# Last attention of a graph network layer on one core: GpSimd adds the probabilities of two units, and TensorE takes their sums over sources once for both

## The reference

```python
H, D = (8, 32)                                   # heads, features of a head
h = (feat @ W.T).reshape(N, H, D)
e = einsum('ehd,ehd->eh', h[src], h[dst]) / sqrt(D)
m = segment_max(e, dst, num_segments=N)
ex = exp(e - m[dst])
s = segment_sum(ex, dst, num_segments=N)         # the sum over sources
out = segment_sum(h[src] * (ex / s[dst])[:, :, None], dst, num_segments=N)
```

## Time and profile before

| what | value |
|---|---|
| median of 3 runs | 6491.18 us |
| the profiled execution, its own time | 6495.75 us |
| its span | 6493.9 us |
| TensorE busy, of the span | 5235.9 us (81%) |
| VectorE | 3690.0 us (57%) |
| ScalarE | 1601.6 us (25%) |
| GpSimd | 3034.0 us (47%) |
| the last attention in the trace | 5424 to 6137 us |

### The profile page before, as it was taken

One profiled execution on the slowest core, in us unless ns is written; L12 is line 12 of the kernel. 1 busy time (PEld: TensorE's weight loads), 2 busy tenths in 40 slices (PEclk: granted clock), 3 DMA queues, 4 the chain that ended last, 5 costly groups with the idle time before them and its releaser, 6 DMA issues.

```text
span 6493.9 us, 83030 instructions
## 1 busy us (share of the span) xinstructions
PE 5235.9 (81%) x25932; PEld 3282.1 (51%) x25932; DVE 3690.0 (57%) x7654; ACT 1601.6 (25%) x2625; POOL 3034.0 (47%) x2048
## 2 busy tenths in 40 slices
PE   4677777777699898989569798776657998998899
PEld 3555555555455575558557566761113333222366
DVE  6777777787511202120235400979986997777732
ACT  1111111111222201220132121245541003555421
POOL 2577777788888878877777885000000000000000
PEclk8887887788799988999788699989988999999889
DMA  7765565644555596559799766944340001222100
GB/s 172 171 119 109 110 120 114 94 65 64 57 20 15 8 124 41 15 23 125 90 159 112 56 48 61 206 105 120 105 115 28 28 24 46 72 73 70 53 17 25
DMA packets 537605, 515.96 MB, mean 79 GB/s; under 512 B 262861, under 2 KB 494230, under 8 KB 531390
## 3 DMA queue, kind: packets, MB, share of 16 engines
q1 hardware_dynamic: 275694, 422.98, 29.8%
q0 software_dynamic: 261696, 90.13, 22.6%
HBM read 359.18 MB, written 153.71 MB: 79 GB/s over the span
## 4 chain that ended last, share of the span: by engine, by line
PE 46%; DVE 13%; issue 6%; SPq 5%; DMA 3%; ACT 1%; DVEq 0%; POOL 0%; ACTq 0%; POOLq 0%; PEldq 0%
PE PS L909 6%; PE PS L881 6%; PE PS L2033 6%; SPq L187 5%; PE PS L1901 5%; DVE WORK L1785 4%; PE PS L1270 4%; DVE MXS L1942 4%; PE PS L892 4%; PE PS L1562 3%; PE PS L1061 2%; PE PS L1050 2%; PE PS L245 2%; PE PS L1922 1%; PE PS L1252 1%
## 5 line engine op out<-in xcount | busy, mean ns | idle before, releaser
L642 POOL DMA_INDIRECT pairs<-PAIR_CNT,PAIR_IDX x1364 | 2159.8, 1583 | 559.1 <-issue 438.9
L469 DVE SCALAR_TENSOR_TENSOR XT<-PS,ROWS,XT 128x512 f32<-128x512 f32 (+1 forms) x1364 | 937.6, 743 | 148.1 <-PE PS L461 137.7
L999 DVE SCALAR_TENSOR_TENSOR X<-PS,G,X 125x256 f32<-125x256 f32 x440 | 193.0, 479 | 827.0 <-PE PS L909 786.2
L682 POOL DMA_INDIRECT sums<-WORK,ROWS x340 | 529.7, 1558 | 251.4 <-issue 189.0
L2088 DVE SCALAR_TENSOR_TENSOR WORK<-WORK 125x1000 f32<-125x1000 f32 x400 | 462.1, 1197 | 203.9 <-ACT WORK L2063 199.5
L1901 PE MATMUL PS<-ROWS 32*125 32x500 f32 x3200 | 455.8, 639 | 28.8 <-DVE MXS L1942 19.2
L1942 DVE TENSOR_REDUCE MXS<-PS 125x4 f32<-125x2000 f32 x200 | 438.8, 2235 | 41.6 <-PE PS L1922 37.6
L2063 ACT ACTIVATE WORK<-PS 125x1000 f32<-125x1000 f32 x400 | 380.0, 1002 | 329.3 <-PE PS L2023 329.3
L510 PE MATMUL PS<-WORK,IDENT 125*125 125x256 f32 x680 | 257.6, 467 | 237.9 <-DMA WORK<-x_table,WORK 237.7
L461 PEld LDWEIGHTS PS<-IDENT,ROWS 128*128 128x128 f32 (+1 forms) x2728 | 434.1, 226 | 30.0 <-issue 0.7
L461 PE MATMUL PS<-IDENT,ROWS 128*128 128x128 f32 (+1 forms) x2728 | 433.4, 312 | 0.0
(11 more groups left out here) (284 smaller groups left out, 7438.5 us busy)
## 6 DMA issues: line engine op xcount, KB each, us to landing
WORK<-pairs SPq DMA_DIRECT2D x400, 218.8 KB
pairs<-ROWS SPq DMA_DIRECT2D x75, 976.6 KB
WORK<-pairs SPq DMA_DIRECT2D x48, 1093.8 KB
WORK<-pairs SPq DMA_DIRECT2D x80, 546.9 KB
pairs<-PAIR_CNT,PAIR_IDX POOLq DMA_INDIRECT x1364
WORK<-pairs SPq DMA_DIRECT2D x40, 382.8 KB
XT<-pairs SPq DMA_DIRECT2D x12, 1093.8 KB
mask_t<-ROWS SPq DMA_DIRECT2D x40, 273.4 KB
```

The lines of the kernel that those rows point to most:

```text
L469: st.go(dve.scalar_tensor_tensor(KEY_JUNK[0:n, q, 0:SUPER * n], PS[0:n, bank, 0:SUPER * n], cols[0:n, q:q + 1], weights, ALU.is_equal, ALU ...
L642: pool.indirect_dma_start(table, bass.IndirectOffsetOnAxis(idx[:, n:n + 1], 0), cnt[:, n:n + 1], None, compute_op=ALU.add).then_inc(sem(do ...
L682: pool.indirect_dma_start(sums[c], bass.IndirectOffsetOnAxis(SROW[:, k % 8:k % 8 + 1], 0), SUMMED[:, k % 8, :], None, compute_op=ALU.add). ...
```

## The change

GpSimd gets a third part to its program, `l3_att_pool`. For each pair i of units (2i and 2i + 1, both of one group) it waits until VectorE has multiplied all four halves (`l3a_prob` 4i + 4), and adds the 2000 columns of the one unit to those of the other, into one of two new buffers `E3_PAIR` that lie in rows 4 and 5 of `ROWS` (f32, 125 x 2000, operands and result in SBUF). It raises `l3a_pair`.

TensorE's `values(n)` keeps only the four matmuls with `Y256`. The four matmuls with ones run once for each pair, on the sum (`pair_sums`), and come later: those of pair i stand behind `values` of unit 2i + 3; those of the last pair of a group stand right behind that pair's own values, after those of the pair before.

ScalarE waits in addition for `l3a_pair` before it overwrites a buffer that GpSimd reads; VectorE's `divide` waits in addition for the sums (`l3a_summed`). The names that GpSimd uses are made semaphores of their own, since it takes no part in the stages.

```diff
-          "gathered", "codes_ready", "outs_loaded", ...
+          "gathered", "codes_ready", "l3a_p", "l3a_summed", "outs_loaded", ...
...
+        E3_UNIT = [flat(WORK, q * 4 * CH, 4 * CH)[0:P] for q in range(4)]
+        E3_PAIR = [flat(ROWS[:, 4:6].rearrange("p a b -> p (a b)"), q * 4 * CH, 4, CH)[0:P] for q in range(2)]
+
+        def l3_att_pool(pool):
+            for i in range(NC * T):
+                pool.wait_ge(sem("l3a_prob"), 4 * i + 4)
+                if i >= 2:
+                    pool.wait_ge(sem("l3a_summed"), i - 1)
+                pool.tensor_tensor(E3_PAIR[i % 2].rearrange("p g n -> p (g n)"), E3_UNIT[2 * i % 4],
+                                   E3_UNIT[(2 * i + 1) % 4], ALU.add).then_inc(sem("l3a_pair"), 1)
...
             def values(n):
                 m, c, t = unit(n)
                 pe.wait_ge(sem("l3a_prob"), 2 * n + 2)
-                for bank in (SUM_BANK, ONE_BANK):
-                    for g in range(G4):
-                        lhsT = Y256[:, t, m * 128 + DH * g:m * 128 + DH * g + DH] if bank == SUM_BANK else ONES_32
-                        ins = pe.matmul(PS[group(g), bank, 0:CH], lhsT, E3[(2 * n + g // 2) % 8][:, g % 2, :],
-                                        start=t == 0, stop=t == T - 1, skip_group_check=True)
+                for g in range(G4):
+                    ins = pe.matmul(PS[group(g), SUM_BANK, 0:CH], Y256[:, t, m * 128 + DH * g:m * 128 + DH * g + DH],
+                                    E3[(2 * n + g // 2) % 8][:, g % 2, :], start=t == 0, stop=t == T - 1,
+                                    skip_group_check=True)
                 ins.then_inc(sem("l3a_used"), 1)
+                if n % 2:
+                    if n // 2 % HT2:
+                        pair_sums(n // 2 - 1)
+                    if n // 2 % HT2 == HT2 - 1:
+                        pair_sums(n // 2)
+
+            def pair_sums(i):
+                pe.wait_ge(sem("l3a_pair"), i + 1)
+                for g in range(G4):
+                    ins = pe.matmul(PS[group(g), ONE_BANK, 0:CH], ONES_32, E3_PAIR[i % 2][:, g, :],
+                                    start=i % HT2 == 0, stop=i % HT2 == HT2 - 1, skip_group_check=True)
+                ins.then_inc(sem("l3a_summed"), 1)
...
                 if n >= 4:
                     act.wait_ge(sem("l3a_used"), n - 3)
+                    act.wait_ge(sem("l3a_pair"), n // 2 - 1)
...
             def divide(k):
                 dve.wait_ge(sem("l3a_used"), T * (k + 1))
+                dve.wait_ge(sem("l3a_summed"), HT2 * (k + 1))
...
             edges_pool(pool)
             pairs_pool(pool)
+            l3_att_pool(pool)
```

More of the change, by code:

```diff
@@ L51 @@
           "pairs_coded", "pairs2_added",
-          "gathered", "codes_ready", "outs_loaded", "params_loaded", "ahead_loaded", "edge_added", "sum_kept", "edge_coded")
+          "gathered", "codes_ready", "l3a_p", "l3a_summed", "outs_loaded", "params_loaded", "ahead_loaded", "edge_added", "sum_kept", "edge_coded")
 def build(nc, a, out):
```

## The result

The change makes the kernel slower: 6710.31 us (median of 4 runs, 6703.24 to 6716.65) against 6487.81 us of the kernel before in the same comparison. The ratio is 1.0347, with a 95% interval from 1.0327 to 1.0367. Forecast were 6765 us and a range from 6500 to 6900.

The account below looks back on a forecast made before the run. TensorE's matmuls were taken as the bound inside a group, 6.15 us a pair. Terms 327 - 57 + 4 = +274 us on the profiled 6495.75 gave 6770, or 6765 against the runs' median 6491.18; range 6500 to 6900.

Parts of the forecast that it names:

- The engines take turns, whole instruction by whole instruction: Inside a group, VectorE's multiplications and GpSimd's add never overlap: 9.42 us a pair against 6.15; chance 0.66.
- Faster: Rival: both engines run side by side and the add is short; -72 us, 6419 us; chance 0.17.
- no change: Rival: first exponential or loads come later than thought, a pair stays near 6.15 us; 6490 us; chance 0.02.
- long P without sharing: Rival: engines run side by side, GpSimd's long add bounds each pair; with 8 us an add, 6660 us; chance 0.07.
- Finer sharing: Rival: engines share finer than by instruction, 1.05 ns an element, 8.4 us a pair; 6660 us; chance 0.08.
- P, the add: One GpSimd f32 add of 125 x 2000, two SBUF operands: taken as 4.8 us, bounded by 2.39 and 13.1.
- Four multiplications, 4.62: VectorE's unchanged work for a pair of units: 2 x 2.31 = 4.62 us.
- Pairs: 100 pairs in the last attention, each 9.42 us instead of 6.15: +3.27 each, +327 us.
- Changes of group, -57: Nine group ends: 4.64 us of add hidden beside the division, VectorE's idle 1.75 us shorter; 9 x 6.4 = -57 us.
- earlier restart: At a change of group, sums no longer precede the next scores, so VectorE's idle 6.38 us shrinks by 1.75.
- TensorE's saving: Matmuls by ones done once a pair, not twice: 5.43 us instead of 6.15, 72 us for 100 pairs if nothing else is late.
- The clock: TensorE's clock may fall in its pauses: counted at nothing; +106 us in the worst case, at its lower level throughout.

Follow-up runs that it names:

- the operand in PSUM: Changed kernel without matmuls by ones, transposes in bank 6; multiplication's second operand from PSUM: 6382.04 us; control with it from SBUF: 6698.92 us.
- adds that nobody waits for: Kernel before, plus 100 GpSimd adds of 2000 columns on buffers of its own that nobody reads: 6726.13 us, ratio 1.0365.
- the pieces: Changed kernel with the same GpSimd add cut in four adds of 500 columns: 6737.90 us, ratio 1.0381 to the kernel before.
- the kernel with 8 columns: Changed kernel, but GpSimd adds only the first 8 of 2000 columns, all waits and matmuls kept: 6411.04 us, ratio 0.9901.

## Why the prediction was right, step by step

- *The engines take turns, whole instruction by whole instruction* (given 0.66). Shown: by the operand in PSUM (6382 against 6699), by adds that nobody waits for (1.0365), by the sizes (a pair of 6.57 and 8.69 with adds of 2.3 and 4.4), by the held multiplication, which ends 1.06 us after the add, and by the pieces, which alternate. The Trainium skill, SBUF — State Buffer, section "Who interferes with whom", says that a VectorE instruction with two SBUF inputs contends with a GpSimd instruction that reads SBUF, and not with one that only writes it. This case agrees in both: multiplications of up to 5508 ns beside adds and 2893 beside copies, and of at most 1203 beside memsets.
- *The rivals.* "Faster" and "no change" fall with the held multiplications, and long P without sharing with P = 4.41. Finer sharing was put at 8.4 us a pair and 6660 us, so near the measured 8.69 and 6710 that the time can't tell it from whole turns; the trace can, since with it every multiplication beside an add would be somewhat longer, while 310 of them take 1.19 us and 90 carry the whole add. Besides, its 1.05 ns a column isn't what the row gives: 1197 ns for 1000 columns are 1.2, and with that it would be 9.6 a pair.
- *P, the add.* Taken as 4.8, measured 4.41 alone. By this term the sum was 0.4 a pair, 40 us, too high. The Trainium skill, GPSIMD Engine Reference, section "Elementwise — side-by-side cycle accounting", gives 4497 ns for 2048 columns; the estimate from it, 4.39, is within 1% of the 4.41 measured.
- *Four multiplications, 4.62.* Measured 8.69 - 4.40 = 4.29. Back to back one costs 1.11, four 4.44, so 4.62 counted the end of each couple twice. The other 0.15 appears only where GpSimd hands over, and what it consists of wasn't separated. 33 us too high.
- *Pairs.* +2.54 each, 254 us, where 327 were forecast; so the distance from reciprocal to reciprocal rose to 93.8 us, and not to the 99 named as the sign.
- *Changes of group, -57.* This step failed. Ten pairs of 8.69 are 86.9, and the groups are 93.4 to 93.8 long (the last one aside), so a change costs 6.8 us against 9.95 before, -3.2 each, -28 in all. I took the hidden add (4.64) and the earlier restart (1.75) off the old 9.95. But that was counted against TensorE's 6.15 a pair, and in turns VectorE sets the time. VectorE's own change before was 4.64 + 0.68 and 6.4 to 6.6 idle, 11.7 to 11.9. Now it is 4.64 + 0.68 and 5.1 to 5.5 idle, less the add of 4.45 beside the division; in five of nine changes another 0.3 to 0.85 idle follow behind the next two multiplications. That makes 6.65 in the mean, of the measured 6.8. The hidden add was seen rightly; what it was taken from was not.
- *The earlier restart* came to about 1.1 us in place of 1.75. In the kernel before, at the change of the earlier trace rows, values and sums ran at a granted clock of 0.50, the lower level of 1.2 GHz, behind TensorE's idle time, and the clock rose within the scores after them (mean 0.78, the window of the kernel before below). In the kernel after, with no sums in between, the scores themselves still ran at 0.50, 1.98 us of them at the change at 5798.72 (the last line below). From the scores' start to the exponential it was 1.73 us (5508.24 to 5509.97) and is 2.30 (5798.72 to 5801.02), so of the 1.8 us of sums that are gone 0.6 went back.
- *End, +4.* VectorE was idle 5.73 us before the last division, against 2.0: +3.7.
- *Sum.* 254 - 28 + 4 = 230 with the measured terms, against 222.5 in the medians and 223.6 in the stage of the two traces; the 6 or 7 us in between are not pinned down. The two errors ran against each other, 73 us too many for the pairs and 29 us too much taken off at the changes. That the total came within 55 us is in part luck; the sign and the mechanism are not.
- *TensorE's saving* of 72 us was right in size, as the kernel with 8 columns shows (64, interval 45 to 83). In the changed kernel none of it shows in the time, within the noise.
- *The clock.* The granted clock of the stretch fell from 0.93 to 0.84, as the window of the kernel after shows against the earlier trace rows, while TensorE's busy time rose by only 11 us with 800 fewer instructions. It stayed beneath VectorE's time, as forecast.

```profile
5415.00:6350.00 935.00, 661.95 (x4824) 176.25 (x4824) 873.50 (x438) 378.81 (x399) 516.79 (x100) 0.84 0.19 54
```

The change of group for the earlier restart, a window of the kernel before and the chain of the kernel after:

```profile
5508.20:5510.00 1.80, 1.80 (x20) 0.81 (x20) 0.00 (x0) 0.03 (x1) 0.00 (x0) 0.78 0.00 0
```

```profile
5796.83 1.89 PE PS L2042 x8
5798.72 1.98 PE PS L1901 x8
```

## What to carry to other kernels

An idle GpSimd is not free capacity beside a VectorE that works with two SBUF operands: what GpSimd reads, it reads in VectorE's time, so add its work to VectorE's and compare the sum with the bound. Here 4.29 + 4.41 stood against 6.15, and the 0.72 us forecast as TensorE's gain could not show inside a group. Where one of VectorE's operands lay in PSUM, or GpSimd only wrote, the multiplications kept their 1.19 us.

And where the bound moves to another engine, count every part of the loop, the changes of group too, in the time of the new bound.

## What the runs showed of the hardware

- An f32 add on GpSimd with both operands in SBUF takes 202 ns for 8 columns, 1.23 us for 500, 2.31 for 1000 and 4.41 for 2000 where nothing holds it: about 0.2 us and 2.1 ns a column. A copy of 2000 columns takes 1.85 us, a memset 1.77.
- Neither engine is starved: with work waiting on both, they alternate one instruction each. With one add behind four multiplications that costs 0.93 us of waiting inside the add and some 4.3 inside one multiplication; with pieces of 500 columns every multiplication waits for a piece (median 2242 ns), and three of four pieces wait for a multiplication (median 2201).
- The hand-over itself costs nothing that shows; a pair is even a little shorter than both engines' work alone, with four multiplications at 1.11 us: 8.69 against 4.44 + 4.41 = 8.85 with one add, 6.57 against 4.44 + 2.31 = 6.75 with 1000 columns, 7.75 against 4.44 + 3.70 = 8.14 with two copies, 8.9 against 4.44 + 4.92 = 9.36 with four pieces. That is 0.1 to 0.2 us less for each instruction of GpSimd that holds a multiplication.
- A VectorE instruction with at most one SBUF operand did not wait for the adds: the reciprocal takes 3278 ns in both kernels, with an add of 4.45 us beside nine of the ten in the changed one.
